# Expert products in groups of 512 tokens, with a transposed first product and rows turned by VectorE

## The chip, the cores and the metric

The kernel runs on one core of a Trainium2 chip. The metric is the device time of one execution in microseconds. Before the change it is 1199.97 us, the median of three runs (1203.39, 1199.97, 1197.99).

## What is computed

Two residual layers act on x, 8 batches of 512 tokens with 512 features, all in float32. The first (L0) makes a low-rank correction of a base matrix from a condition vector per batch and adds x times that matrix. The second (L1) is a mixture of experts: each token goes through a shared gated FFN (inner width 1024) and through two of eight experts (width 512), chosen by a router.

```
x  = x + L0(x)                                # 4096 tokens x 512
shared = silu(xf @ w1) * (xf @ w3) @ w2       # inner width 1024
s = sigmoid(concat(xf, tf) @ router_W)
topk_idx = top_k(s + router_bias, 2)          # gates: the two s, divided by their sum
h = gelu(xf @ W1e[e]);  y = h @ W2e[e]        # for each expert e, width 512
x = x + (shared + sum over 2 of gate * y) / 3
```

The router's bias is drawn with a spread of 1.126 and differs between experts by more than a sigmoid can; so two experts are chosen for all 4096 tokens. The kernel is written for any routing and reads the counts at run time.

## The kernel before, in words

All products run at float32 quality as three passes of TensorE: each operand is cut into a high part (a cast by ScalarE) and a low part (operand minus high part, by VectorE), and high x high, high x low and low x high are added in PSUM. That is `mm3`, L1375 to L1377; every product below has 3 matmuls for each 128 of its inner dimension, and two "cuts" for each operand.

Stages in order of time:
1. The L0 layer, batches 0 to 7, with the router beside it. Its result x1 is kept turned (features on partitions, `xp`) and is turned back by TensorE; `keep_tok` on ScalarE writes it as rows (`x1tok`). SP stores these rows in `x1_d`; GpSimd scatters each token's row twice into `xs_d`, one region per expert, in the order of the tokens (indirect DMAs, L701).
2. The shared FFN of the last batch (`ffn(S, ...)`), in 8 pieces h of 128 inner columns: 12 matmuls for U, 12 for V, and 12 for the sums of the piece before. Beside it VectorE makes the tables of tiles (`tables`, `rows_in_ys`, `gate_weights`), after its pieces 3 to 5. They go to a DRAM tensor and back into one partition, `tab_i`, from which the engines read registers (`value`).
3. The experts' tiles: 128 tokens of one expert each, as many as the counts need (a loop over pairs). SP fills up the rows of each expert's last tile with zeros (L577) ahead of it. Per tile: SP loads 128 rows of `xs_d` (L588, two buffers); TensorE turns them (`tx`, L1660, 4 transposes); ScalarE and VectorE cut them; TensorE multiplies them with the first weights, rows as the stationary operand (12 matmuls of 512 columns); ScalarE applies Gelu; TensorE turns the result (`th`, L1703, 4 transposes); both cut it; TensorE multiplies with the second weights (12 matmuls); VectorE copies the result out (L1297); SP stores it in `ys_d` (L604). GpSimd loads and cuts each active expert's weights once, ahead of its tiles, into one of two slots (`cut_expert`, L722 to L728).
4. The shared FFN of batches 0 to 6 in a loop (`ffn(F, ...)`). Beside it GpSimd gathers the two expert rows of each token (L752), and VectorE adds, in place in `xres`: x1 + shared/3 (`add_shared`) + gate x expert row twice (`add_expert`). SP stores the block. The last batch's sum, whose shared part is still in PSUM, is formed first.

Each engine executes its program in order and waits on semaphores at each instruction. PSUM banks `K[0]`, `K[1]`, `L`, `Rb` hold turned tiles and both products of stage 3; `M[0..3]` keep the last batch's shared sums meanwhile. Nothing plans the order at run time; it is as the code has it.

## Time and profile before

| | |
|---|---|
| median of 3 runs | 1199.97 us |
| profiled execution: time / span | 1202.75 us / 1200.9 us |
| TensorE busy | 1160.2 us (97%) |
| VectorE / ScalarE / GpSimd busy | 416.4 / 287.8 / 188.1 us |
| data moved | 151.82 MB, mean 126 GB/s |
| granted TensorE clock, mean | 0.985 of full speed |

The span is the time on the chip's engines, the time also holds what lies around it. A busy TensorE is not TensorE at its best: matmuls overlap, and the time from start to start tells what one costs. An engine's idle time counts only where something on the path waits for it.

### The profile page before, as it was taken

What the parts mean: (1) busy time and instruction counts of PE and PEld (TensorE: products, weight loads), DVE (VectorE), ACT (ScalarE), POOL (GpSimd) and SP (SyncE); (2) the same over time, 40 slices, a digit from 0 to 9 for tenths busy, and PEclk for the clock granted to TensorE, in tenths of its full rate; (3) what the DMA queues carried; (4) which work ended last, traced back from release to release, by engine and by line L of the source; (5) the groups of instructions that cost most, each with busy time, mean ns of one, the idle gap of its engine ahead of it and who ended that gap; (6) DMA issues with size and microseconds to landing.
All of it is one profiled execution on the core that took longest, in us unless ns stands there. A gap on an engine that the chain in (4) does not pass through costs nothing.

```text
span 1200.9 us, 18241 instructions
## 1 busy us (share of the span) xinstructions
PE 1160.2 (97%) x5762; PEld 935.4 (78%) x5763; DVE 416.4 (35%) x812; ACT 287.8 (24%) x498; POOL 188.1 (16%) x207
## 2 busy tenths in 40 slices
PE   6999898899999999999999998999999999999998
PEld 5666676778788888888888887888888888888887
DVE  4104653535233333333333334233333314233334
ACT  2212453521222222222222222121211112121211
POOL 2002165642510000000000003202020010202020
PEclk8999999899999999999999999999999999999999
DMA  8562589895332222222222224404031130404031
GB/s 309 227 239 95 207 299 347 289 306 162 129 118 83 79 87 79 79 87 79 82 84 83 83 79 123 175 1 175 1 100 74 39 136 0 175 0 175 0 125 49
DMA packets 70480, 151.82 MB, mean 126 GB/s; under 512 B 9753, under 2 KB 18457, under 8 KB 68658
## 3 DMA queue, kind: packets, MB, share of 16 engines
q1 hardware_dynamic: 57666, 111.55, 26.9%
q0 software_dynamic: 12784, 39.86, 9.4%
q8 instruction: 20, 0.33, 0.1%
q14 instruction: 10, 0.08, 0.0%
HBM read 88.73 MB, written 62.65 MB: 126 GB/s over the span
## 4 chain that ended last, share of the span: by engine, by line
PE 91%; DVE 4%; DMA 2%; POOL 1%; issue 1%; ACT 1%; SPq 0%; DVEq 0%; ACTq 0%
PE L L1375 7%; PE L L1377 7%; PE L L1376 7%; PE Rb L1377 7%; PE Rb L1375 7%; PE Rb L1376 7%; PE M L1375 5%; PE M L1376 5%; PE M L1377 5%; PE K L1376 5%; PE K L1375 5%; PE K L1377 5%; PE Rb L1465 3%; PE K L1703 2%; PE K L1660 2%; PE M L1403 2%
## 5 line engine op out<-in xcount | busy, mean ns | idle before, releaser
L752 POOL DMA_INDIRECT yb<-ys_d,pos_fix x64 | 61.2, 957 | 326.6 <-DVE xres L1324 308.6
L1375 PE MATMUL L<-weh,xgh 128*128 x260 | 107.6, 414 | 1.8 <-issue 1.8
L1276 DVE TENSOR_TENSOR xgl<-K,xgh 128x512 fp32r<-128x512 f32 x66 | 45.7, 692 | 173.4 <-ACT xgh L897 173.4
L1375 PE MATMUL Rb<-weh,hTh 128*128 x256 | 105.5, 412 | 0.0
L1375 PE MATMUL K<-x1h,w13h 128*128 128x512 f32 x256 | 101.6, 397 | 3.0 <-DVE x1l L1355 3.0
L1375 PE MATMUL M<-w2h,gTh 128*128 128x512 f32 x256 | 102.3, 399 | 2.3 <-DVE gTl L460 2.3
L1377 PE MATMUL L<-weh,xgl 128*128 x260 | 102.7, 395 | 0.0
L1376 PE MATMUL L<-wel,xgh 128*128 x260 | 102.5, 394 | 0.0
L1376 PE MATMUL K<-x1l,w13h 128*128 128x512 f32 x256 | 102.0, 398 | 0.0
L1376 PE MATMUL M<-w2l,gTh 128*128 128x512 f32 x256 | 101.9, 398 | 0.0
L1377 PE MATMUL M<-w2h,gTl 128*128 128x512 f32 x256 | 101.8, 398 | 0.0
L1377 PE MATMUL K<-x1h,w13l 128*128 128x512 f32 x256 | 101.7, 397 | 0.0
L1377 PE MATMUL Rb<-weh,hTl 128*128 x256 | 100.5, 393 | 0.0
L1376 PE MATMUL Rb<-wel,hTh 128*128 x256 | 100.2, 391 | 0.0
L445 ACT ACTIVATE slf<-K 128x512 f32<-128x512 f32 x64 | 38.3, 599 | 238.3 <-PE K L1377 234.2
L448 ACT CAST gTh<-slf 128x512 fp32r<-128x512 f32 x64 | 39.7, 621 | 191.7 <-DVE slf L458 191.7
L458 DVE TENSOR_TENSOR slf<-L,slf 128x512 f32<-128x512 f32 x32 | 22.1, 692 | 169.2 <-PE L L1377 162.5
L905 ACT CAST hTh<-K 128x512 fp32r<-128x512 f32 x65 | 38.2, 587 | 163.9 <-PE K L1703 163.9
L1297 DVE COPY yo<-Rb 128x512 f32<-128x512 f32 x64 | 44.3, 692 | 92.2 <-PE Rb L1377 92.2
L701 POOL DMA_INDIRECT xs_d<-x1tok,pos_int x64 | 68.2, 1065 | 38.0 <-issue 24.6
L901 ACT ACTIVATE hg<-L 128x512 f32<-128x512 f32 x65 | 38.9, 598 | 146.5 <-PE L L1377 146.5
L746 POOL COPY pos_fix<-ypos 128x8 int32 (+1 forms) x8 | 2.3, 283 | 442.6 <-DMA ys_d<-yo 390.0
(238 smaller groups left out, 2146.1 us busy)
## 6 DMA issues: line engine op xcount, KB each, us to landing
xr<-xs_d SPq DMA_DIRECT2D x68, 256.0 KB, 2.6
w2c<-in_L_cond_w_dram SPq DMA_DIRECT2D x8, 2048.0 KB, 8.5
ys_d<-yo SPq DMA_DIRECT2D x64, 256.0 KB, 2.1
xtok<-in_x_dram SPq DMA_DIRECT2D x32, 256.0 KB, 7.4
x_d<-x1tok SPq DMA_DIRECT2D x8, 1024.0 KB, 7.9
xres<-x_d SPq DMA_DIRECT2D x8, 1024.0 KB, 9.5
x1T_d<-xp SPq DMA_DIRECT2D x7, 1024.0 KB, 4.6
out_dram<-xres SPq DMA_DIRECT2D x7, 1024.0 KB, 4.8
```

The costliest lines, as they stand in the source:

```text
L445: nc.scalar.activation(slf[:, h % 2], U[h % 2][:], ACT.Silu).then_inc(ffn.silu, 1)
L448: nc.scalar.copy(gTh[:, h % 2], slf[:, h % 2]).then_inc(ffn.g_hi, 1)
L701: pool.indirect_dma_start(out=xs_d, out_offset=bass.IndirectOffsetOnAxis(ap=pos_int[:, c:c + 1].bitcast(U32), axis=0), in_=x1tok[i][:, t, ...
L752: pool.indirect_dma_start(out=yb[:, c, :], out_offset=None, in_=ys_d, in_offset=bass.IndirectOffsetOnAxis(ap=pos_fix[:, c:c + 1].bitcast(U ...
L901: nc.scalar.activation(hg[:], HP[:], ACT.Gelu).then_inc(h_g, 1)
L905: nc.scalar.copy(hTh[:].rearrange("p k n -> p (k n)"), TH[:]).then_inc(ht_hi, 1)
L1276: tt(xgl[:].rearrange("p k n -> p (k n)"), TX[:], xgh[:].rearrange("p k n -> p (k n)").bitcast(F32), ALU.subtract).then_inc(xg_lo, 1)
L1297: nc.vector.tensor_copy(yo[:, s], YP[:]).then_inc(y_sb, 1)
L1375: mm(o, ah, bh_, start=start, stop=False)
L1376: mm(o, ah, bl_, start=False, stop=False)
L1377: return mm(o, al, bh_, start=False, stop=stop)
L1465: last_mm = mm(Rb[32 * q:32 * q + 32, cc * P:(cc + 1) * P], hTz[:, k, 2 * j + part], w[:, k, 2 * q + j], start=(n == 0 and j == 0 and k == 0),
```

## The change

Stage 3 takes groups of 512 tokens (`GR`) instead of tiles of 128; regions, padding, tables and `ys_d` follow that size (`LAST` is the number of groups less one). For each group both weights of its expert are loaded whole by SP (1 MB each) and cut in four pieces by ScalarE and VectorE, also when the expert stays the same. The first product has the weights as stationary operand and all 512 tokens as moving one, so its result is already turned, four pieces of 128 hidden values in four banks; Gelu goes to `hg` in SBUF and is cut from there. The second product takes 128 tokens as stationary operand, in two halves of two banks. TensorE turns nothing in this stage. Instead `keep_tok` writes each row in the order (j, c, f) of its features (quarter j of every 128), SP loads quarter j of 512 rows onto partitions 32j to 32j+31 (four DMAs), and VectorE's 32x32 transposes of such a tile give features on partitions. ScalarE copies results out (`keep_y`). SP issues the padding of the regions after the tables; GpSimd zeroes the part of `ys_d` that groups may leave unwritten (7 groups) once the first weights are in. The final sums go to a tile of their own, `total`; the first add of each reads `xres` in the changed order, in four parts. In `tables` 17 operations stand where 35 did. ScalarE's and VectorE's cuts of the first group's first weights stand after piece 6 of stage 2.

```
+    GR = TT * P
+    REGION = N + GR
...
+        def groups(eng, body):
+            last = value(eng, LAST, 0, GROUPS_MAX - 1, 1)
+            with eng.Fori(0, last) as g:
+                body(g, g + 1)
+            body(last, None)
+            return last
...
+            pad_src = zeros[:].unsqueeze(1).broadcast_to([P, GR * D // (P * P), P])
+                row = value(sp, PAD, e, E * REGION - GR)
+                sp.dma_start(xs_d[ds(row, GR), :].rearrange("(p r) (k c) -> p (r k) c", p=P, c=P), pad_src).then_inc(pad_out, 16)
...
+            def load_e1(g):
+                row = value(sp, EROW, g, (E - 1) * KC)
+                sp.dma_start(e1raw[:], w1e_view[:, ds(row, KC), :]).then_inc(e1_in, 16)
...
+            def load_rows(g):
+                row = value(sp, ROW, g, E * REGION - GR)
+                rows = xs_d[ds(row, GR), :].rearrange("(n t) (j f) -> j t n f", t=32, j=4)
+                for j in range(4):
+                    sp.dma_start(xr[32 * j:32 * j + 32].rearrange("p t i f -> p (t i) f"), rows[j]).then_inc(xr_in, 16)
+            def store_y(g, s):
+                sp.wait_ge(y_sb, g * TT + (2 * s + 2 + Y_FREE))
+                alone(sp)
+                sp.dma_start(ys_d[ds(g * GR + s * (GR // 2), GR // 2), :].rearrange("(t p) d -> p t d", p=P),
+                             yo[:, 2 * s:2 * s + 2]).then_inc(y_out[s], 16)
...
+            load_e1(0)
+            sp.wait_ge(pad_out, 16 * E)
+            load_rows(0)
+            load_e2(0)
+            def load_group(g, n):
+                if n is not None:
+                    sp.wait_ge(e1_lo, n * KC)
+                    load_e1(n)
+                    sp.wait_ge(xt_f, n * TT)
+                    load_rows(n)
+                    sp.wait_ge(e2_lo, n * KC)
+                    load_e2(n)
+                else:
+                    sp.wait_ge(xt_f, g * TT + TT)
...
+                    sp.dma_start(xres[:], x1_view[:, (NB - 1) * TT:NB * TT, :]).then_inc(xres_in, 16)
+                    sp.wait_ge(h_ps, g * KC + KC)
+                    sp.wait_ge(xg_lo, g * TT + TT)
+                    alone(sp)
+                    sp.dma_start(x1raw[:], x1T_d[:, 0:1, :].rearrange("p b n -> p (b n)")).then_inc(x1raw_in, 16)
+                sp.wait_ge(ys_zero, 16 * (GROUPS_MAX - SURE))
+                store_y(g, 0)
+                store_y(g, 1)
...
+            pool.wait_ge(e1_in, 16)
+            zero_src = zeros[:].unsqueeze(1).broadcast_to([P, GR * D // (P * P), P])
+            for g in range(SURE, GROUPS_MAX):
+                pool.dma_start(ys_d[g * GR:(g + 1) * GR, :].rearrange("(p r) (k c) -> p (r k) c", p=P, c=P), zero_src
+                               ).then_inc(ys_zero, 16)
...
-                nc.scalar.copy(x1tok[TOK_BUFFER[b]][:, t], k_bank("t", b, t)[:]).then_inc(tok_sb, 1)
+                nc.scalar.copy(x1tok[TOK_BUFFER[b]][:, t].rearrange("p (j c f) -> p c j f", j=4, c=KC),
+                               k_bank("t", b, t)[:].rearrange("p (c j f) -> p c j f", j=4, c=KC)).then_inc(tok_sb, 1)
...
+            def cut_e1(g, m):
+                act.wait_ge(e1_in, g * 16 + 16)
+                if not first(g):
+                    act.wait_ge(h_ps, g * KC - KC + m + 1)
+                cols = slice(m * P, (m + 1) * P)
+                nc.scalar.copy(e1h[:, :, cols], e1raw[:, :, cols]).then_inc(e1_hi, 1)
+            def cut_e2(g, m):
+                act.wait_ge(e2_in, g * 16 + 16)
+                act.wait_ge(y_ps, g * TT + Y_FREE)
+                nc.scalar.copy(e2h[:, m], e2raw[:, m]).then_inc(e2_hi, 1)
+            def cut_x(g, t):
+                act.wait_ge(xt_f, g * TT + t + 1)
+                if first(g):
+                    act.wait_ge(S.v_ps, HC)
+                else:
+                    act.wait_ge(h_ps, g * KC)
+                nc.scalar.copy(x1h[:, :, t * P:(t + 1) * P], xt[:, t % 2]).then_inc(xg_hi, 1)
+            def gelu(g, m):
+                act.wait_ge(h_ps, g * KC + m + 1)
+                act.wait_ge(ht_lo, g * KC + (m - 1 + H_FREE))
+                nc.scalar.activation(hg[:, m % 2], G[m][:], ACT.Gelu).then_inc(h_g, 1)
+                act.wait_ge(h_g, g * KC + m + 1)
+                act.wait_ge(y_ps, g * TT + Y_FREE)
+                nc.scalar.copy(hTh[:, m], hg[:, m % 2]).then_inc(ht_hi, 1)
+            def keep_y(g, t):
+                act.wait_ge(y_ps, g * TT + (t + 1 + Y_FREE))
+                act.wait_ge(y_out[t // 2], g * 16 + YO_FREE)
+                nc.scalar.copy(yo[:, t], G[t][:]).then_inc(y_sb, 1)
...
+            after[HC - 2] = lambda: [cut_e1(0, m) for m in range(KC)]
+            ffn_act(act, S, 0, True, after)
+            act.sem_inc(y_sb, Y_FREE)
+            for t in range(TT):
+                cut_x(0, t)
...
+            def pass_group(g, n):
+                cut_e2(g, 0)
+                cut_e2(g, 1)
+                gelu(g, 0)
+                cut_e2(g, 2)
+                gelu(g, 1)
+                cut_e2(g, 3)
+                if n is not None:
+                    cut_e1(n, 0)
+                gelu(g, 2)
+                if n is not None:
+                    cut_e1(n, 1)
+                gelu(g, 3)
+                if n is not None:
+                    cut_x(n, 0)
+                    cut_e1(n, 2)
+                    cut_x(n, 1)
+                    cut_e1(n, 3)
+                    cut_x(n, 2)
+                    cut_x(n, 3)
+                keep_y(g, 0)
+                keep_y(g, 1)
+                if n is None:
+                    act.wait_ge(x1raw_in, 16)
+                    act.wait_ge(h_ps, g * KC + KC)
+                    cut_x1(0)
+                keep_y(g, 2)
+                keep_y(g, 3)
+            last = groups(act, pass_group)
...
+            def turn_rows(g, t):
+                dve.wait_ge(xr_in, g * 64 + 64)
+                if not (first(g) and t < 2):
+                    dve.wait_ge(xg_lo, g * TT + (t - 1))
+                nc.vector.transpose(xt[:, t % 2].rearrange("p c (i n) -> p i c n", i=4),
+                                    xr[:, t].rearrange("p i (c f) -> p i c f", c=KC)).then_inc(xt_f, 1)
+            def cut_x(g, t):
+                dve.wait_ge(xg_hi, g * TT + t + 1)
+                cols = slice(t * P, (t + 1) * P)
+                tt(x1l[:, :, cols], xt[:, t % 2], x1h[:, :, cols].bitcast(F32), ALU.subtract).then_inc(xg_lo, 1)
...
+            def pass_group(g, n):
+                cut_e2(g, 0)
+                cut_e2(g, 1)
+                cut_h(g, 0)
+                cut_e2(g, 2)
+                cut_h(g, 1)
+                cut_e2(g, 3)
+                if n is not None:
+                    turn_rows(n, 0)
+                    cut_e1(n, 0)
+                cut_h(g, 2)
+                if n is not None:
+                    turn_rows(n, 1)
+                    cut_e1(n, 1)
+                cut_h(g, 3)
+                if n is not None:
+                    cut_x(n, 0)
+                    cut_e1(n, 2)
+                    turn_rows(n, 2)
+                    cut_x(n, 1)
+                    cut_e1(n, 3)
+                    turn_rows(n, 3)
+                    cut_x(n, 2)
+                    cut_x(n, 3)
+            last = groups(dve, pass_group)
...
+            def fused(t, part, scale, n, done_):
+                if n is not None:
+                    dve.wait_ge(acc, n)
+                    ins = nc.vector.scalar_tensor_tensor(out=total[:, t], in0=part, scalar=scale, in1=total[:, t],
+                                                         op0=ALU.mult, op1=ALU.add)
+                else:
+                    for j in range(4):
+                        ins = nc.vector.scalar_tensor_tensor(
+                            out=total[:, t].rearrange("p (c j f) -> p j c f", j=4, c=KC)[:, j],
+                            in0=part.rearrange("p (c j f) -> p j c f", j=4, c=KC)[:, j], scalar=scale,
+                            in1=xres[:, t].rearrange("p (j c f) -> p j c f", j=4, c=KC)[:, j],
+                            op0=ALU.mult, op1=ALU.add)
+                ins.then_inc(done_, 1)
...
-            def tx(t, slot):
-                pe.wait_ge(xr_in[slot], ((t - slot) >> 1) * 16 + 16)
-                pe.wait_ge(xg_lo, t)
-                for k in range(KC):
-                    last_mm = nc.tensor.transpose(TX[:, k * P:(k + 1) * P], xr[:, slot, k * P:(k + 1) * P], ident[:])
-                last_mm.then_inc(xg_ps, 1)
...
-            def th(t):
-                pe.wait_ge(h_g, t + 1)
-                pe.wait_ge(ht_lo, t)
-                for k in range(KC):
-                    last_mm = nc.tensor.transpose(TH[:, k * P:(k + 1) * P], hg[:, k * P:(k + 1) * P], ident[:])
-                last_mm.then_inc(ht_ps, 1)
...
+            def mm1(g):
+                pe.wait_ge(xg_lo, g * TT + TT)
+                for m in range(KC):
+                    pe.wait_ge(e1_lo, g * KC + m + 1)
+                    pe.wait_ge(y_sb, g * TT + (m - TT + 1 + Y_FREE))
+                    cols = slice(m * P, (m + 1) * P)
+                    for k in range(KC):
+                        last_mm = mm3(G[m][:], e1h[:, k, cols], e1l[:, k, cols], x1h[:, k], x1l[:, k], k == 0, k == KC - 1)
+                    last_mm.then_inc(h_ps, 1)
+            def mm2(g):
                 for s in range(2):
+                    for m in range(KC):
+                        if s == 0:
+                            pe.wait_ge(ht_lo, g * KC + (m + 1 + H_FREE))
+                            pe.wait_ge(e2_lo, g * KC + m + 1)
+                        for t in (2 * s, 2 * s + 1):
+                            if m == 0:
+                                pe.wait_ge(h_g, g * KC + t + 1)
+                            rows = slice(t * P, (t + 1) * P)
+                            last_mm = mm3(G[t][:], hTh[:, m, rows], hTl[:, m, rows], e2h[:, m], e2l[:, m], m == 0, m == KC - 1)
+                            if m == KC - 1:
+                                last_mm.then_inc(y_ps, 1)
...
```

`load_e2`, `cut_e1`, `cut_e2` and `cut_h` on VectorE follow the same pattern (high part awaited, then one subtraction). SP's `load_group` for the last group loads `xres` and the first block's input instead of a next group.

## Rows read from the trace of the kernel before

**Rows 1.** Page, part 4: chain that ended last, share of the span by engine.
```profile
PE 91%; DVE 4%; DMA 2%; POOL 1%; issue 1%; ACT 1%; SPq 0%; DVEq 0%; ACTq 0%
```

**Rows 2.** Windows: length, busy of PE, PEld, DVE, ACT, POOL; PEclk, DMA share, GB/s.
```profile
0.00:244.30 244.30, 214.18 (x1432) 166.04 (x1434) 95.17 (x294) 80.96 (x141) 82.78 (x110) 0.95 0.70 253
244.30:305.70 61.40, 59.10 (x248) 46.99 (x247) 29.16 (x80) 14.57 (x21) 25.19 (x18) 0.97 0.66 213
305.70:725.50 419.80, 414.72 (x2069) 343.14 (x2068) 135.00 (x196) 109.47 (x198) 16.65 (x8) 1.00 0.27 88
725.50:1200.90 475.40, 472.19 (x2016) 379.24 (x2016) 157.07 (x243) 82.83 (x139) 63.48 (x72) 1.00 0.24 84
```

**Rows 3.** Timeline of PE in the tiles: start us, us, engine line op.
```profile
600.56 0.60 PE L1703 MATMUL K<-ident,hg 128*128 128x128 f32 x4
603.76 0.60 PE L1660 MATMUL K<-ident,xr 128*128 128x128 f32 x4
604.11 0.48 PE L1375 MATMUL Rb<-weh,hTh 128*128 x1
606.95 0.60 PE L1703 MATMUL K<-ident,hg 128*128 128x128 f32 x4
```

**Rows 4.** Groups by line, PE: count | busy, mean ns | idle before.
```profile
L1660 PE MATMUL K<-ident,xr 128*128 128x128 f32 x264 | 39.4, 271 | 0.0
```

**Rows 5.** Timeline of PE in the first FFN block.
```profile
732.75 0.40 PE L1375 MATMUL K<-x1h,w13h 128*128 128x512 f32 x1
735.55 0.40 PE L1375 MATMUL Rb<-x1h,w13h 128*128 128x512 f32 x1
```

**Rows 6.** Timeline of PE: idle before in brackets, and the matmuls behind it.
```profile
311.80 0.49 PE L1375 MATMUL L<-weh,xgh 128*128 x1 [1.83 <-issue]
313.32 0.63 PE L1377 MATMUL L<-weh,xgl 128*128 x1
313.75 0.63 PE L1375 MATMUL L<-weh,xgh 128*128 x1
725.53 0.58 PE L1375 MATMUL K<-x1h,w13h 128*128 128x512 f32 x1 [3.02 <-DVE x1l L1355]
```

**Rows 7.** Timeline of ACT and PE at the end of the shared FFN.
```profile
291.76 0.62 ACT L448 CAST gTh<-slf 128x512 fp32r<-128x512 f32 x1 [3.02 <-DVE slf L458]
302.83 0.50 PE L1375 MATMUL M<-w2h,gTh 128*128 128x512 f32 x1 [0.28 <-DVE gTl L460]
```

**Rows 8.** Timeline of DVE: first and last of 35 operations of the tables.
```profile
267.80 0.16 DVE L956 SCALAR_TENSOR_TENSOR tw<-iota,taken 128x8 f32<-128x8 f32 x1
274.67 0.17 DVE L996 CAST tabi<-tab 128x8 int32<-128x8 f32 x1
```

**Rows 9.** SP timeline; windows: zeros alone, long rows; DMA issues with landing.
```profile
278.78 14.04 SPq L577 DMA_DIRECT2D xs_d<-zeros  x8
...
270.00:271.00 1.00, 1.00 (x6) 0.82 (x5) 0.83 (x6) 0.00 (x0) 0.00 (x0) 1.00 0.97 288
298.00:299.00 1.00, 1.00 (x6) 0.82 (x5) 0.00 (x0) 0.00 (x0) 0.00 (x0) 1.00 1.01 406
...
xs_d<-zeros SPq DMA_DIRECT2D x9, 256.0 KB, 3.4
```

**Rows 10.** DMA issues: count, KB each, us from issue to landing.
```profile
weraw<-in_L_cond_W1e_dram POOLq DMA_DIRECT2D x2, 1024.0 KB, 6.0
```

**Rows 11.** Groups by line: ACT Gelu, DVE subtraction, DVE 32x32 transposes.
```profile
L901 ACT ACTIVATE hg<-L 128x512 f32<-128x512 f32 x65 | 38.9, 598 | 146.5 <-PE L L1377 146.5
...
L1276 DVE TENSOR_TENSOR xgl<-K,xgh 128x512 fp32r<-128x512 f32 x66 | 45.7, 692 | 173.4 <-ACT xgh L897 173.4
L1165 DVE STREAM_TRANSPOSE zz<-L 32x128 f32<-32x128 f32 x32 | 10.0, 313 | 0.6
```

**Rows 12.** Timeline of DVE at the last block's seventh piece.
```profile
1186.08 5.39 DVE L1324 SCALAR_TENSOR_TENSOR xres<-yb,gate_fix,xres 128x512 f32<-128x512 f32 x8
1192.22 0.69 DVE L458 TENSOR_TENSOR slf<-Rb,slf 128x512 f32<-128x512 f32 x1 [0.75 <-PE Rb L1377]
```

More of the change, by code:

```diff
@@ L950, in tables @@
             tt, ts, red = nc.vector.tensor_tensor, nc.vector.tensor_scalar, nc.vector.tensor_reduce
-            cnt, nt, active, ends, ranks, past, rows, t7, t8, t9 = (tw[:, i] for i in range(10))
-            col = [tab[:, i:i + 1] for i in range(8)]
-            tmp = [tw[:, 10, i:i + 1] for i in range(4)]
-            ti = [twi[:, 1, i:i + 1] for i in range(4)]
+            cnt, nt, ends, past, rows, t9 = (tw[:, i] for i in (0, 1, 2, 3, 4, 9))
+            col = [tab[:, i:i + 1] for i in range(COLS)]
@@ L960, in tables @@
             link(nc.vector.tensor_copy(nt, twi[:, 0]))
[L961 removed]
             link(nc.vector.tensor_tensor_scan(ends, ones[:, 0:E], nt, 0.0, ALU.mult, ALU.add))
[L963 removed]
             link(ts(past, ends, iotap[:, 0:1], None, ALU.is_le))
[L966 removed]
+            link(red(tmp[1], past, AX, ALU.add))
```

353 lines of the change are left out of this document (113 added, 240 removed).

## The prediction, made before the changed kernel ran

> **What bounds the kernel now.** I read the chain of waits first: 91% of the path to the end is TensorE [rows 1]. The windows then cut the span by stage: everything ahead of the shared FFN takes 244.3 us, the shared FFN 61.4, the expert tiles 419.8 and the seven FFN blocks behind them 475.4 [rows 2]. TensorE is busy in 414.7 of the 419.8 us of the expert stage, VectorE in 135, ScalarE in 109, and the DMA engines are a quarter used. So in this stage only what TensorE itself executes, or a wait put in front of it, moves the end.
>
> The timeline of TensorE in that stage shows the tile: from one group of turned hidden values (L1703) to the next are 6.39 us [rows 3], and the stage issues 64 of these tiles (the 64 stores of one tile each, and 264 input transposes with the two tiles read ahead [rows 4], say the same). Inside a tile are 24 matmuls of 512 columns and 8 transposes of 128 columns; four transposes hold the engine 0.35 us (603.76 to 604.11, [rows 3]). In the FFN blocks the same form of matmul, weights at a fixed address, comes every 0.2333 us (12 from 732.75 to 735.55, [rows 5]). GpSimd loaded and cut weights for two experts only (two loads of each kind, [rows 10]). Two experts with 64 full tiles are 4096 tokens each, thus 8 groups of 512 each, 16 groups with no padding; other routing would cost a part group per expert.
>
> **The change, part by part.** The sum is made against the profiled execution: 1200.9 us span, 1202.75 us time, so 1.85 us lie outside the span. That run is 2.8 us over the median of the runs shown, 1199.97.
>
> *Removed from TensorE: the transposes.* The input rows are turned by VectorE, and a first product with the weights stationary gives hidden values already turned. The number of 512-column matmuls stays: per group 48 and 48, in all 16 x 96 = 1536. At 0.2333 us that is 22.4 us a group and 358.4 us in all. The tiles' matmuls run a little closer inside a tile, 24 in 6.39 - 2 x 0.35 = 5.69 us with the joints, 0.237 each, so no loss is taken; if the new ones came every 0.2275 us, the sum would be 9 less. Stage before 419.8, now 358.4: 61.4 saved at most. Of that 50 are the transposes' 64 x 0.79, 2.8 the 65th first product that ran ahead for nothing, 3.0 the wait at the stage's end, 1.8 one near its start, and two stretches of about 8 matmuls after these at a spacing of 0.43 us (granted clock at the lower level, [rows 6]), 1.6 each.
>
> *Added ahead of the stage: 8 MB of zero rows.* Each expert's end is padded with 512 rows instead of 128, for all eight experts, and the first group's rows wait for it; before, 2 MB. The tables are ready at 274.8 [rows 8]; they lose some 18 of their 35 links of 0.2 us, so 271.2 now. From there to the first pad were 3.9 us [rows 8, 9]: first pad at 275.1. Zero rows move in 512-byte pieces, and where they have the engines for themselves these carry 288 GB/s at a full share [rows 9]. 8 x 1,048,576 bytes take 29.1 us. A 256 KB zero store lands 3.4 us after its issue, of which 0.9 is data, so 2.5 on top: 306.7. SP issues the load of the first weights only behind this, on the same queue: 2.6 us more at the 406 GB/s of a load with long rows [rows 9], so 309.3.
>
> Now the queues behind that wait. ScalarE is told to cut these weights between the shared FFN's seventh and eighth piece, that is after 292.4 [rows 7]; it waits 17 us, and its Silu of the eighth piece stands behind. Four casts of 0.6, then Silu, product, cast, subtraction: 309.3 + 2.4 + 0.6 + 0.7 + 0.6 + 0.7, with the gaps 315.1. TensorE, which went on at 302.8 before (waiting 0.28 only [rows 7]), has its last 12 matmuls of this stage at 315.1, at the lower clock until 320.2. Meanwhile SP waits for the pads, loads the rows (1 MB; they share the engines with 7 MB of zeros that GpSimd now starts), landing about 316.5; four turns, casts and subtractions in sequence at 0.69 with hand-overs take 5.9: the first expert matmul at 322.4, against 305.7. That is 16.7 us lost, and 1.6 for the clock. Bounds: nothing, if the pads are quicker than I think or the wait lies elsewhere; 25 us, if GpSimd's zeros take half of the engines from the rows all the time.
>
> *The loop.* ScalarE has 24 instructions of 0.6 us a group and VectorE 20 of 0.7: 14.4 and 14 us of 22.4 [rows 11], covered if the order fits. I follow one group, its first product at 0: pieces of hidden values come at 2.8, 5.6, 8.4 and 11.2; the second product starts at 11.2 and wants the third and fourth piece at 14.0 and 15.4. On VectorE "turn rows of the next group, cut a weight piece" stands twice ahead of these (turn, cut, cut_h, turn, cut, cut_h): from the landing of the rows the two cut_h end after 2.1 and 4.1 us. So rows have to be there by 11.3, or TensorE waits for the difference. SP reaches the loads only after the store of the previous group's last half, about 1.4, reads a register, and issues the weights at about 2.7. A 1 MB weight load landed 6.0 us after issue [rows 10]: 8.7; the rows stream behind it, 3.6 us at 288 GB/s: 12.3. With less neighbouring traffic than that load had, 10.8. I take 12.0, a wait of 0.7 us, in 15 groups 10.5 us. Ends: zero; and if each of the four quarter loads needs the 1.75 us at which 256 KB zero stores followed each other (14.04 us for eight [rows 9]), 7.0 in place of 3.6, a wait of 4.4.
> The turn is priced from the VectorE transpose that the trace has, 0.313 us for 128 columns on 32 partitions [rows 11]: 0.69 if it streams like a subtraction of 512 columns, 1.25 if four times the small one. The nearer row is the subtraction of the same size; at 1.25 the second cut_h is 1.1 later, which belongs into the same range.
> The row view shows full-partition zeros at 288 GB/s; no row shows a large transfer on 32 partitions, which is what each quarter load is. The Trainium skill, "SBUF — State Buffer", section "Door 1: The DMA port swizzle", says that a transfer over 32 partitions reaches 8 of 16 ports, and gives 189 GB/s for 1 MiB against 328 over all. By the page's figure the rows would stream in 5.5 us instead of 3.6 (an estimate), a wait of 2.6 a group and 39 us in place of 10.5.
>
> *Zeros of GpSimd.* 7 MB of zeros and 4 MB of loads share the engines from 309 on; at 288 GB/s that ends near 348, and the first result store (about 342), with the loads of group 2 behind it on SP, waits for that: 1 us. The two weight loads per group in place of two in all raise the traffic from 88 to about 190 GB/s, well under the 406 seen; TensorE does not see it but for the above.
>
> *The end of the stage and the blocks.* Input for the first FFN block is loaded and cut during the last second product, so the 3.0 us wait goes, and the clock does not fall: the blocks take 475.4 - 1.6. The first add of each sum goes in four parts (16 instructions of 0.28 for 4 of 0.69): 2 us more on VectorE, hidden under 5.6 us of products, but in the last block VectorE's sums of 5.39 become about 7.2 where only 0.75 us were free [rows 12]; 1.1 late, of which TensorE has 0.4 of slack: 0.7. The reordered write of the turned tokens, and 2 MB of zeros that SP no longer issues earlier, I cost at nothing: GpSimd's scatter sets that stretch.
>
> *Sum:* 1200.9 - 61.4 + 16.7 + 1.6 + 10.5 + 1.0 - 1.6 + 0.7 = 1168.4; plus 1.85 is 1170.3, against 1202.75; from the median of 1199.97 the same step gives **1167**.
>
> **The rivals.**
> A. *The pads do not hold the start.* 18.3 us come back, 1149, and with no wait in the loop 1138. For it: the eight pads of before landed within 3.4 us each. Against it: 29 us of bytes in a stretch of 27 us.
> B. *The rows come late in every group.* Each us of landing past 11.3 is one of TensorE, 15 times. If the row load takes 5.5 us, between the 3.6 and the 7.0 above, it lands at 13.9, the wait is 2.6 and the 15 cost 28.5 us more than my 10.5: 1196. With half of that excess, 1181. For it: single buffers for rows and weights, loaded only after the previous store. Against: the DMA engines have a quarter of their time in use now [rows 2] and half then. The page of the Trainium skill named above would make this the case.
> C. *The same, and the clock falls each time*: the slower side. After a wait of 1.8 us TensorE ran 8 matmuls at 0.43 instead of 0.23 [rows 6], 1.6 us. From the point where one wait in a group is 1.8 us, a group loses 3.4 and 15 lose 51: without my 10.5 the sum is 1156.6, so 1208, and more beyond; the four loads at 1.75 us would give 4.4 + 1.6 = 6.0 a group and 1247. For it: nothing shows a quarter load's price. Against: the lateness splits over two pieces of hidden values, and each wait must be long by itself; waits of 0.25 to 0.28 us left the clock at the higher level.
> D. *The change does not take the work off TensorE*, if the first product with stationary weights needed more matmuls: excluded by the code, 48 for 48.
>
> **How the numbers follow.** Forecast 0.45 (1155 to 1178), A 0.15, B 0.27, C 0.13. A difference under 0.5%, 6 us, can't be told from none here. C is slower in most of its part (0.09), within 0.5% in the rest (0.02), to which B's far end adds 0.04: same 0.06, slower 0.09, faster 0.85. The range from 1143 to 1200 leaves out a part of A and C.
>
> **What would show it.** Right: no 128-column transposes of TensorE in the stage; first expert matmul near 322 with ScalarE waiting for the weights' DMA from 292 to 309; groups every 23.1 us with VectorE's turn waiting for the row DMA; no wait of 3 us before the first block. Wrong: a first expert matmul before 310, a turn far from 0.69 us, groups over 24 us, a fallen clock inside the loop.

## The result, and the profile after

The changed kernel took 1213.41 us (median of 4, 1211.64 to 1215.86) beside 1200.96 for the kernel before on the same chip (4 runs, 1197.99 to 1203.39). The ratio is 1.0106, with a 95% interval from 1.0075 to 1.0137: a little slower. Forecast were 1167 us, in a range that ended at 1200; rival C, the slower side, had 1208. The profiled execution spans 1212.4 us.

Part 4 of the page after, the chain that ended last, and three groups of part 5 (count | busy, mean ns | idle before and who ended it):
```profile
PE 67%; DMA 14%; SPq 7%; DVE 7%; issue 4%; ACT 2%; DVEq 0%; ACTq 0%
...
L1445 PE MATMUL M<-w2h,gTh 128*128 128x512 f32 x256 | 102.2, 399 | 16.0 <-DVE gTl L475 16.0
L1445 PE MATMUL K<-e2h,hTh 128*128 128x512 f32 x128 | 58.8, 460 | 55.0 <-DVE hTl L1318 54.3
L1298 DVE STREAM_TRANSPOSE xt<-xr 128x512 f32<-128x512 f32 x64 | 45.1, 705 | 109.3 <-DMA xr<-xs_d 109.1
```
TensorE had 91% of the path before [rows 1] and has 67% now; DMA has 14%. The transposes of TensorE are gone, and VectorE's turn of a tile costs 0.705 us, as taken. But TensorE idles 54.3 us in the groups of the experts in front of the second product, in 15 stretches, and 16 us ahead of the first group; VectorE idles 109 us for the row load.

The stages after, to be held against [rows 2] (length, busy of PE, PEld, DVE, ACT, POOL; PEclk, DMA share, GB/s):
```profile
0.00:244.00 244.00, 217.58 (x1456) 168.61 (x1457) 99.46 (x299) 84.23 (x146) 84.66 (x115) 0.97 0.72 260
244.00:303.00 59.00, 48.16 (x208) 38.71 (x206) 17.43 (x54) 8.35 (x13) 5.97 (x8) 0.94 0.80 237
303.00:741.00 438.00, 376.98 (x1549) 302.03 (x1550) 205.35 (x336) 221.36 (x391) 7.98 (x7) 0.93 0.62 170
741.00:1212.40 471.40, 467.88 (x2016) 378.64 (x2015) 160.35 (x328) 82.69 (x138) 62.84 (x72) 1.00 0.24 84
```
The third window, the expert stage with the last matmuls of the shared FFN, holds 520 fewer matmuls than before and TensorE is busy 37.7 us less in it, yet it is 18 us longer. Its granted clock is 0.93 instead of 1.00.

**The start.** Timeline of SyncE (SP), ScalarE and TensorE around the pads (start us, us, engine, line; in brackets the idle time before and who ended it):
```profile
266.31 24.87 SPq L586 DMA_DIRECT2D xs_d<-zeros  x8
293.58 1.29 SPq L597 DMA_DIRECT2D e1raw<-in_L_cond_W1e_dram  x1
298.99 1.94 SPq L608 DMA_DIRECT2D xr<-xs_d  x4
...
302.63 2.18 ACT L904 CAST e1h<-e1raw 128x512 fp32r<-128x512 f32 x4 [20.11 <-DMA e1raw<-in_L_cond_W1e_dram]
...
307.81 0.80 PE L1445 MATMUL M<-w2h,gTh 128*128 128x512 f32 x1 [15.66 <-DVE gTl L475]
314.47 0.47 PE L1445 MATMUL K<-x1h,e1h 128*128 128x512 f32 x1 [1.17 <-DVE x1l L1304]
```
The first expert matmul comes 53.0 us after the tables (261.48); I had 322.4 - 271.2 = 51.2. The 24.9 us are SyncE's issuing; the zero rows themselves move at 284 GB/s from 268 to 292, so 8 MB take 29.5 us.

**Group 0.** GpSimd's zeros, the row load of group 1 (SyncE) and the turn that waits for it:
```profile
302.90 8.08 POOL L736 DMA_DIRECT2D ys_d<-zeros  x7 [51.20 <-DMA e1raw<-in_L_cond_W1e_dram]
...
313.86 8.95 SPq L608 DMA_DIRECT2D xr<-xs_d  x4
...
341.04 0.71 DVE L1298 STREAM_TRANSPOSE xt<-xr 128x512 f32<-128x512 f32 x1 [18.26 <-DMA xr<-xs_d]
```
The rows of group 1 need 27 us from the first issue to the turn, and TensorE waits 14.7.

**A later group**, g = 5; SyncE, VectorE and TensorE (first the matmul that opens the group), then windows between the landings:
```profile
455.83 4.38 SPq L613 DMA_DIRECT2D ys_d<-yo  x2
462.07 0.40 SPq L597 DMA_DIRECT2D e1raw<-in_L_cond_W1e_dram  x1
463.39 2.16 SPq L608 DMA_DIRECT2D xr<-xs_d  x4
...
473.64 0.71 DVE L1298 STREAM_TRANSPOSE xt<-xr 128x512 f32<-128x512 f32 x1 [6.64 <-DMA xr<-xs_d]
474.27 0.65 DVE L1309 TENSOR_TENSOR e1l<-e1raw,e1h 128x512 fp32r<-128x512 f32 x1
474.84 0.68 DVE L1318 TENSOR_TENSOR hTl<-hg,hTh 128x512 fp32r<-128x512 f32 x1
...
458.78 0.39 PE L1445 MATMUL K<-x1h,e1h 128*128 128x512 f32 x1
...
475.58 0.50 PE L1445 MATMUL K<-e2h,hTh 128*128 128x512 f32 x1 [3.04 <-DVE hTl L1318]
...
465.00:467.00 2.00, 2.00 (x11) 1.65 (x10) 1.29 (x2) 1.16 (x3) 0.00 (x0) 1.00 1.02 357
467.00:469.00 2.00, 2.00 (x11) 1.65 (x10) 0.00 (x0) 0.81 (x2) 0.00 (x0) 1.00 1.19 199
469.00:471.00 2.00, 2.00 (x10) 1.67 (x9) 0.00 (x0) 1.94 (x4) 0.00 (x0) 1.00 1.24 196
```
This is the order that the prediction followed: store, weights, rows, turn, cut of a weight piece, cut of hidden values. The turn of the rows starts 14.9 us after the group does (14.65 on average over the groups behind group 0); 11.3 were needed, and TensorE waits 3.04. While the weights load the engines move 357 GB/s; while only rows load, 196 to 199 with the engines shown just as full.

Behind such a wait the clock falls in nine of the groups 1 to 14 and stays in five (2, 5, 8, 10 and 13). Group 4 is one of the nine; the rows are TensorE's timeline (spacing 0.23 us before, 0.43 after), a window of two of these microseconds, and the windows of groups 4 and 5 as a whole:
```profile
448.60 0.50 PE L1445 MATMUL K<-e2h,hTh 128*128 128x512 f32 x1 [2.66 <-DVE hTl L1318]
...
451.84 0.63 PE L1445 MATMUL K<-e2h,hTh 128*128 128x512 f32 x1
452.27 0.63 PE L1446 MATMUL K<-e2l,hTh 128*128 128x512 f32 x1
...
451.00:453.00 2.00, 2.00 (x6) 1.61 (x5) 2.00 (x4) 0.62 (x1) 0.00 (x0) 0.50 0.00 0
432.18:458.78 26.60, 23.85 (x98) 18.91 (x96) 12.45 (x20) 13.68 (x25) 0.00 (x0) 0.94 0.56 158
458.78:484.33 25.55, 22.36 (x97) 17.86 (x96) 12.45 (x20) 13.56 (x25) 0.00 (x0) 1.00 0.59 152
```
The granted clock is 0.50 from 451 to 453, the lower of the two levels. The nine groups with such a stretch take 26.5 us on average and the five without it 25.3, so the fall costs 1.2 us each time, 11 us in all.

### The profile page after: what moved, and what is told of

It is laid out like the page before. It is cut to its first block, busy times and chain, and to the rows that moved or that the text cites. A ratio compares the mean times of both kernels' runs of the same rounds, so it can differ in the third digit from the quotient of the medians.

```text
span 1212.4 us, 15385 instructions
## 1 busy us (share of the span) xinstructions
PE 1110.6 (92%) x5226; PEld 888.0 (73%) x5226; DVE 482.6 (40%) x1015; ACT 396.6 (33%) x687; POOL 161.4 (13%) x200
## 4 chain that ended last, share of the span: by engine, by line
PE 67%; DMA 14%; SPq 7%; DVE 7%; issue 4%; ACT 2%; DVEq 0%; ACTq 0%
DMA xr<-xs_d 12%; PE K L1445 7%; PE K L1446 6%; PE K L1447 6%; PE M L1445 4%; PE M L1446 4%; PE M L1447 4%; PE L L1445 4%; PE L L1446 4%; PE L L1447 4%; PE Rb L1446 3%; PE Rb L1445 3%; PE Rb L1447 3%; SPq L419 3%; PE Rb L1535 3%
## 5 line engine op out<-in xcount | busy, mean ns | idle before, releaser
L1445 PE MATMUL K<-e2h,hTh 128*128 128x512 f32 x128 | 58.8, 460 | 55.0 <-DVE hTl L1318 54.3
L1298 DVE STREAM_TRANSPOSE xt<-xr 128x512 f32<-128x512 f32 x64 | 45.1, 705 | 109.3 <-DMA xr<-xs_d 109.1
L1445 PEld LDWEIGHTS K<-e2h,hTh 128*128 128x128 f32 x128 | 27.4, 214 | 70.7 <-DVE hTl L1318 65.3
L917 ACT CAST x1h<-xt 128x512 fp32r<-128x512 f32 x64 | 39.7, 620 | 115.1 <-DVE xt L1298 115.1
L1445 PEld LDWEIGHTS M<-w2h,gTh 128*128 128x128 f32 x256 | 48.6, 190 | 28.6 <-DVE gTl L475 16.8
L1314 DVE TENSOR_TENSOR e2l<-e2raw,e2h 128x512 fp32r<-128x512 f32 x64 | 42.6, 687 | 64.0 <-ACT e2h L909 64.0
L473 DVE TENSOR_TENSOR slf<-Rb,slf 128x512 f32<-128x512 f32 x32 | 22.1, 691 | 114.0 <-PE Rb L1447 114.0
L1318 DVE TENSOR_TENSOR hTl<-hg,hTh 128x512 fp32r<-128x512 f32 x64 | 43.9, 687 | 51.8 <-ACT hTh L925 51.8
L475 DVE TENSOR_TENSOR gTl<-slf,gTh 128x512 fp32r<-128x512 f32 x64 | 44.3, 692 | 47.5 <-ACT gTh L463 47.5
L1473 PE MATMUL M<-xTh,bh 128*128 128x512 f32 x128 | 56.4, 441 | 6.0 <-DVE bl L1129 3.2
```

The source lines that it names most:

```text
L473: nc.vector.tensor_tensor(slf[:, h % 2], V[h % 2][:], slf[:, h % 2], ALU.mult).then_inc(ffn.g_f, 1)
L475: nc.vector.tensor_tensor(gTl[:, h % 2], slf[:, h % 2], gTh[:, h % 2].bitcast(F32), ALU.subtract).then_inc(ffn.g_lo, 1)
L1298: nc.vector.transpose(xt[:, t % 2].rearrange("p c (i n) -> p i c n", i=4), xr[:, t].rearrange("p i (c f) -> p i c f", c=KC)).then_inc(xt_f, 1)
L1314: tt(e2l[:, m], e2raw[:, m], e2h[:, m].bitcast(F32), ALU.subtract).then_inc(e2_lo, 1)
L1318: tt(hTl[:, m], hg[:, m % 2], hTh[:, m].bitcast(F32), ALU.subtract).then_inc(ht_lo, 1)
L1445: mm(o, ah, bh_, start=start, stop=False)
```

## The experiments

"Rest" below is the span from the store of the tables (`tab_d<-tabi`) to the end: it leaves out the part ahead, which differs by chip and execution (runs 7 to 9). It is 926.0 us for the kernel before and 950.9 for the changed one. "Period" is the mean time from one row load to the next over 13 groups behind group 1: 26.09 us in the changed kernel. The kernel before took 1201.94 us in the set of runs 1 to 4, 1215.11 in that of runs 5 to 8, 1217.22 in that of runs 9 to 11 and 1196.08 in that of run 12, so each time is held against the kernel before of its own set. Most edits are in SyncE's program.

**1. Rows over 128 partitions in pieces of 2 KB.** The features then reach the products in another order, so the result is another one; the work is the same.
```
-  rows = xs_d[ds(row, GR), :].rearrange("(n t) (j f) -> j t n f", t=32, j=4)
+  rows = xs_d[ds(row, GR), :].rearrange("(t p) d -> t p d", p=P)
-  sp.dma_start(xr[32 * j:32 * j + 32]..., rows[j])
+  sp.dma_start(xr[:, j].rearrange("p i f -> p (i f)"), rows[j])
```


> The row load is four transfers of 128 rows over all 128 partitions in pieces of 2 KB, instead of four over 32 partitions in pieces of 512 bytes; all else stays, the same bytes move and the same turns run, but the features reach the products in another order (this part of the computation is changed). Theory T1, the quarter loads' low rate holds the loop: the rows stream at the 365 to 400 GB/s of a weight load, 2.7 us instead of 5.5 for 1 MB, so they land some 2.8 us sooner after the group's start (about 11.8 instead of 14.6), TensorE's wait before the second product's third piece falls from 2.7-3.0 us to about 0.5, the clock does not fall inside the loop, groups take about 22.3 us instead of 26.1 and the time is 1213 - 14 x 3.8 = 1160. Rival R1, SyncE's order (the loads queued behind the result store) alone: landing moves by less than 1 us and the time stays above 1195. Rival R2, the order on VectorE or ScalarE: landing moves by 2.8 us but the wait stays above 2 us, time above 1200.

Measured: 1150.46 us (2 runs; ratio to before 0.9588, 0.9516 to 0.9659), rest 887.1, period 22.40. SyncE's row load, VectorE's turn and TensorE's waits:
```profile
459.45 1.97 SPq L608 DMA_DIRECT2D xr<-xs_d  x4
...
466.52 0.71 DVE L1298 STREAM_TRANSPOSE xt<-xr 128x512 f32<-128x512 f32 x1 [3.46 <-DMA xr<-xs_d]
...
PE K L1445 <- DVE hTl L1318: 6.2, 2, 6.0
```
From issue to turn the rows take 7.07 us instead of 10.25 (463.39 to 473.64). The wait is gone but for 6.0 us in group 0 and 0.2 in one other, and the clock stays at the higher level in groups 1 to 15. With the same bytes, order and turns, 64 us of the rest come back, 52 of them in groups 1 to 14: T1.

**2. The same with pieces of 512 bytes.**
```
+  rows = xs_d[ds(row, GR), :].rearrange("(t p) (j f) -> j p t f", p=P, j=4)
+  sp.dma_start(xr[:, :, j], rows[j])
```


> The row load is four transfers over all 128 partitions, each in pieces of 512 bytes as in the changed kernel (the features reach the products in another order; this part of the computation is changed). It tells the number of partitions apart from the size of the pieces. If the 32 partitions are what is slow (T1): streaming at about the 288 GB/s that zero stores of 512-byte pieces have, 3.6 us for 1 MB instead of 5.5, landing 1.9 us sooner, groups about 23.3 to 24 us, time 1170 to 1185. If the 512-byte pieces are what is slow (R3): rows land at about 14.6 us after the group's start as now, groups 26 us, time 1205 to 1215.

Measured: 1170.06 us (0.9751, 0.9679 to 0.9823), rest 907.5, period 23.35.
```profile
470.87 2.22 SPq L608 DMA_DIRECT2D xr<-xs_d  x4
...
479.38 0.71 DVE L1298 STREAM_TRANSPOSE xt<-xr 128x512 f32<-128x512 f32 x1 [4.91 <-DMA xr<-xs_d]
...
PE K L1445 <- DVE hTl L1318: 24.9, 15, 13.3
```
8.51 us from issue to turn here, more than in most groups of this run. On average over groups 2 to 15 it is 10.03 us in the changed kernel, 8.03 here and 7.10 in run 1. So of the 2.9 us between the changed kernel and run 1, the 32 partitions make 2.0 and the short pieces 0.9. The size of the pieces (R3) is not the main cause, and not nothing. Waits of 0.5 to 1.5 us are left in groups 1 to 14, and behind none of them does the clock fall.

**3. No pads.** The eight stores and the wait for them are deleted.

> The eight pad stores (8 MB of zero rows) and the wait for them are left out; this input has full groups only, so nothing else changes. If the pads hold the start (the prediction's step, 16.7 + 1.6 us): ScalarE's cut of the first expert's weights waits no more, the first expert matmul comes at 296 to 300 instead of 314.5 and the time falls by 14 to 18 us, to 1195-1199. If the zeros of GpSimd (7 MB), which then start sooner, take over: less than 8 us gained.

Measured: 1186.75 us (0.989, 0.9818 to 0.9962), rest 924.4: 26.5 us less, more than either case said. The first expert matmul comes 35.7 us after the tables (296.48) instead of 53.0, and in group 0 the row loads are 30.8 us apart (44.3 before), since the zeros of GpSimd start at 272, 30 us sooner. In the loop the waits stay (TensorE's waits; groups 1 to 14 together take 369 us, 366 in the changed kernel):
```profile
PE K L1441 <- DVE hTl L1314: 44.2, 15, 3.4
```
15 waits of 2.9 on average, none of 14.7.

**4. Weights loaded once.** `load_e1(n)` and `load_e2(n)` and their waits are deleted from the pass.

> The weight loads of all groups but the first are left out (the cuts stay, the second expert's tokens are multiplied by the first's weights; this part of the computation is changed): 15 x 2 MB less traffic, and SyncE reaches the row load right after the result store without a 1 MB weight transfer ahead of it. T1 (with the rows behind the weights on the same engines): rows land 2.5 to 3.5 us sooner, the wait before the second product goes below 0.5 us, groups about 22.2 us, time 1155 to 1165. If the quarter loads alone are slow for another reason than what stands ahead of them: landing at about +12, as well, but group 0's loss of 17 us stays in any case, since it comes from the 7 MB of zeros. If ScalarE or VectorE hold the loop: groups stay near 26 us.

Measured: 1151.03 us (0.9592, 0.9511 to 0.9674), rest 887.0, period 21.77. Row load and turn:
```profile
460.88 1.95 SPq L608 DMA_DIRECT2D xr<-xs_d  x4
...
468.34 0.71 DVE L1294 STREAM_TRANSPOSE xt<-xr 128x512 f32<-128x512 f32 x1 [2.55 <-DMA xr<-xs_d]
```
With no weights ahead the quarter loads take 7.46 us (7.51 on average), longer than the 7.10 of run 1 behind 1 MB of weights. It is the sum of the two, weights ahead and a low rate, that is late; taking either away is enough. The groups behind group 0 take 21.8 us; TensorE keeps one wait, 11.7 us in group 0.

**5. Zeros for the results ahead of the shared FFN.** The loop of seven stores moves from GpSimd to SyncE, before `sp.wait_ge(weff_ps, 1)`.

> The 7 MB of zeros for the result rows are issued by SyncE before the shared FFN, where the DMA engines are little used, instead of by GpSimd when the first expert's weights have landed; otherwise the changed kernel. If these zeros, sharing the engines with the loads of group 1 and with the first result store, cause group 0's loss of 17 us (38.9 us instead of 21.8; theory T2): group 0 takes 26 us like the others, TensorE's longest wait inside the loop falls from 14.7 to about 3, time 1213 - 13 to 15 = 1198 to 1200. Rival: the single buffers alone hold group 0 (the same wait as in each later group, plus the first-time order of the queues): less than 3 us gained. If the zeros disturb the conditioning loads where they are now put, up to 5 us are given back.

Measured: 1237.5 us beside 1215.11 for the kernel before on that chip; rest 940.6, 10.3 less than the changed kernel's. TensorE's waits:
```profile
PE K L1445 <- DVE hTl L1318: 44.6, 14, 3.9
...
PE M L1485 <- DMA SB<-xwh_d: 7.6, 1, 7.6
```
The row loads of groups 1 and 2 are 27.8 us apart instead of 44.3, and group 0 takes 21.8 us instead of 39.0, so T2 is right for group 0. The groups behind it ran at a period of 26.7 and gave 7 us of that back. Ahead of the tables TensorE waits 7.6 us for a conditioning load, a wait that the changed kernel does not have and more than I allowed. The time came out 38 us above the forecast, mainly because the tables come at 293.3 instead of 261.5; on this chip they come late in every kernel profiled (283.8 to 293.5).

**6. Loads one pass ahead.**
```
+ sp.wait_ge(e1_lo, KC);  load_e1(1);  sp.wait_ge(xt_f, TT);  load_rows(1)
  def load_group(g, n):
-   sp.wait_ge(e1_lo, n * KC);       load_e1(n)
-   sp.wait_ge(xt_f, n * TT);        load_rows(n)
    sp.wait_ge(e2_lo, n * KC);       load_e2(n)
+   sp.wait_ge(e1_lo, n * KC + KC);  load_e1(n + 1)
+   sp.wait_ge(xt_f, n * TT + TT);   load_rows(n + 1)
    store_y(g, 0);  store_y(g, 1)
```
The loads of the pass before the last reach past the last group and are not used; the last pass waits for them.

> SyncE issues the weight and row loads of group n+1 as soon as their buffers are free in group n, ahead of the stores of group n's results, instead of one pass later behind them; no buffer is added, the same bytes move, the quarter loads stay as they are. If lateness is what counts (T1: rows land 3.3 us too late, whether by their rate or by their start): they now land before the previous group's last third, the wait of 2.7 to 3 us goes in all groups, the clock stays, groups take 21.8 us: 14 x 4.2 = 59 us less, and group 0's loss stays (it comes from the zeros): about 1155. Rival R1a: the loads now meet the result stores and the second expert's weights and are as late as before: time above 1195. Rival R2: the order of VectorE or ScalarE makes the wait: groups stay above 24 us, time above 1185.

Measured: 1178.05 us beside 1215.11 for the kernel before on that chip, ratio 0.9692 (0.9628 to 0.9756); rest 889.1, 61.8 less. SyncE's pass, the window of one group, and TensorE's wait:
```profile
441.19 0.39 SPq L597 DMA_DIRECT2D e1raw<-in_L_cond_W1e_dram  x1
442.51 2.08 SPq L608 DMA_DIRECT2D xr<-xs_d  x4
444.94 2.45 SPq L613 DMA_DIRECT2D ys_d<-yo  x2
455.10 0.40 SPq L601 DMA_DIRECT2D e2raw<-in_L_cond_W2e_dram  x1
...
397.00:419.00 22.00, 22.00 (x99) 18.22 (x98) 12.78 (x21) 13.47 (x24) 0.00 (x0) 1.00 0.67 191
...
PE K L1451 <- DVE hTl L1324: 13.1, 1, 13.1
```
The loads stand ahead of the store, TensorE is busy throughout at full clock, and every group behind group 0 takes 21.76 us. The quarter loads are about as slow as they were (median 7.0 us to land, 7.3 in the changed kernel): what cost was that they came late.

**7 and 8. The kernel before with the other spacing of the experts' regions** (`REGION = N + 4 * P`), **and unchanged.**

> The kernel before with one number changed: the rows set aside for each expert in the scattered tokens are 4608 instead of 4224, as in the changed kernel (9.44 MB instead of 8.65 MB from expert to expert). It asks where the 10 us come from that the changed kernel gains ahead of the expert stage, in code that is nearly the same. If the spacing of the experts' regions makes the scattered writes of GpSimd and the weight loads beside them slower: the wait of TensorE at 213 us falls from 7.1 to about 3.7 and the time falls by 5 to 10 us. If it is the order of the copied tokens (4 parts of rows), the queue of zeros that SyncE no longer has at 256 us, or chance: within 2 us of before in that wait.

> The kernel before, unchanged, profiled once more: how much the part ahead of the expert stage differs from one execution to another. If the 10 us by which the changed kernel's shared FFN ends sooner are chance: the wait at 213 us (7.1 us) and the end of that stage (about 302) move by several us here. If they belong to the change: the wait is 7 us and the end 302 within 1 us.

The ratio of run 7 is 0.9992 (0.9956 to 1.0027). The tables are stored at:
```profile
283.82 0.35 SPq L571 DMA_DIRECT2D tab_d<-tabi  x1
```
in run 7, and in run 8, which is the kernel before word for word:
```profile
293.49 0.35 SPq L571 DMA_DIRECT2D tab_d<-tabi  x1
```
In the trace of before it was 274.87. The rest is 925.5 and 927.2 (926.0 before). So the part ahead of the tables differs by 10 us between two executions on one chip, of kernels whose median times agree, and the rest does not. The spacing does not matter.

**9. The changed kernel again.**

> The changed kernel itself, once more, to be held against the others of this set on the same chip. In the set before, on another chip, the part ahead of the tables (261.5 us in the trace of the changed kernel) took 284 to 294 us in the kernel before and 290 to 293 in versions of the changed one, while all that follows the tables agreed within 2 us with the first chip (926.0, 925.5 and 927.2 us for the kernel before). So: from the tables to the end 951 us within 3, wherever the tables come; before 926. If the changed kernel really gains ahead of the tables, they come about 10 us sooner than in the kernel before here too; if that gain was chance, the ratio is above 1.015.

Measured: 1240.85 us beside 1217.22, ratio 1.0195 (1.0124 to 1.0267); tables at 284.74, rest 952.4, as expected. From the medians, with the rest and the 1.85 us outside the span taken off, the tables stand at 289.4 before and 286.6 after here, and at 273.1 and 260.7 on the first chip. The gain ahead of the tables is thus 12 us there, 3 here, and none between run 6 and its neighbour before. What sets it stays open.

**10. The first weights ahead of the pads** (with the loads of run 6).
```
  load_e1(0)
+ load_e2(0)
+ (the eight pad stores)
  sp.wait_ge(pad_out, 16 * E)
  load_rows(0)
```


> The loads one pass ahead (as in the prefetch version), and the first group's weights are issued ahead of the eight pad stores instead of behind them; correct for any routing. ScalarE's cut of the first weights then waits no more and TensorE's wait of 15.7 us before the end of the shared FFN goes; the first rows still wait for the pads. But GpSimd's zeros start with the weights' landing, 30 us sooner, and share the engines with the pads. T1/T2: 15 MB in a row at 337 GB/s end some 45 us after the tables as pads alone would after 25; first expert matmul 5 to 15 us later than the 53 us after the tables that the changed kernel shows at worst, or 10 us sooner at best; group 0's loss of 13 to 17 us mostly gone. From the tables to the end 889 (prefetch) - 5 to - 20: 870 to 885. Rival: the pads and zeros together hold the start longer than before: above 889.

Measured: 1193.09 us (0.9791, 0.9736 to 0.9846), rest 904.9: the rival. The start of the weights releases GpSimd's zeros into the pads:
```profile
293.59 55.29 SPq L617 DMA_DIRECT2D xs_d<-zeros  x8
...
PE K L1451 <- DVE x1l L1310: 50.1, 1, 50.1
```
55.3 us for the eight issues instead of 24.9, and one wait of 50.1. The 337 GB/s of the expectation is 8 MB over SyncE's 24.9 us of issuing, which end before the data; pads and zeros together moved 283 GB/s from 300 to 350, at which 15 MB take 56 us and not 45. The groups behind take 21.76 us as in run 6.

**11. The same, zeros by SyncE**: four before the shared FFN, three behind the last token store.

> As the version with the first weights ahead of the pads, and the 7 MB of zeros issued by SyncE: four before the shared FFN (the engines idle from 88 to 104 us), three behind the last token store ahead of the tables. Correct for any routing. T2: no wait before the last piece of the shared FFN, first expert matmul about 10 us sooner than with the changed kernel, group 0's loss gone, groups 21.8 us: from the tables to the end 951 - 60 - 14 - 10 = 867 to 872, of which up to 5 us may be given back ahead of the tables by the zeros there. Time 25 to 35 us below the prefetch version. Rival: the zeros delay the conditioning loads or the tables by more than 8 us, so nothing is won over the prefetch version.

Measured: 1168.24 us beside 1217.22, ratio 0.9603 (0.9551 to 0.9656); rest 881.1, where I expected 867 to 872. TensorE's one wait inside this part:
```profile
339.66 0.77 PE L1454 MATMUL K<-x1h,e1h 128*128 128x512 f32 x1 [26.26 <-DVE x1l L1313]
```
59.7 us after the tables: the pads start 11 us after them, not 5, since the tables' own two transfers stand behind zeros and two weight loads stand ahead. This version is faster than both kernels and keeps the pads, which inputs with part groups need.

**12. The same without the eight pads.**

> The version before (loads one pass ahead, first weights first, zeros by SyncE) without the eight pad stores; one 1 MB store of zeros at the end of the last region stays for the row load that runs past the last group. Its output is right for inputs with full groups only, as this one; it shows what the pads cost once all else is mended. If the pads alone hold the first expert matmul at 60 us after the tables: it comes at about 36 us after them, the end of the shared FFN, as in the version without pads, and from the tables to the end 881 - 24 = 857 us. If the three stores of zeros ahead of the tables and the two weight loads now hold the first rows: 865 or more.

Measured: 1119.55 us beside 1196.08 in this set (1217.22 in the set of runs 9 to 11, on a chip of the same number), ratio 0.9357 (0.9334 to 0.938); rest 852.9. The tables are ready on VectorE before SyncE, still issuing zeros, stores them:
```profile
260.64 0.17 DVE L1028 CAST tabi<-tab 128x4 int32<-128x4 f32 x1
...
263.73 4.26 SPq L586 DMA_DIRECT2D tab_d<-tabi  x1
...
296.73 0.47 PE L1451 MATMUL K<-x1h,e1h 128*128 128x512 f32 x1 [2.42 <-DVE x1l L1310]
```
The first expert matmul comes 33.0 us after this store and 35.9 after the tables are ready, so counted from there the rest is 855.8: the pads cost 25 us once all else is mended (28 by the store). Against the kernel before the gain is 76 us; 70 of them lie behind the ready tables, the others in the part ahead, which is not to be counted on.

## Why the prediction was wrong

By its own steps, the profiled execution against the 1168.4 of the sum:

| stretch | predicted | measured | difference |
|---|---|---|---|
| start to the tables | 271.2 | 261.5 | -9.7 |
| tables to the first expert matmul | 51.2 | 53.0 | +1.8 |
| group 0, with the zeros and the clock | 25.7 | 39.0 | +13.3 |
| groups 1 to 14 | 14 x 23.1 = 323.4 | 14 x 26.11 = 365.6 | +42.2 |
| last group and seven blocks | 496.9 | 493.3 | -3.6 |
| sum | 1168.4 | 1212.4 | +44.0 |

- **The step that failed: "the rows stream behind it, 3.6 us at 288 GB/s: 12.3 ... I take 12.0, a wait of 0.7 us".** The mechanism was right, the size was not. The weights landed near the 8.7 us that I had (their cut starts 9.0 us after the group's start on average, 9.4 in group 5); the rows then took 5.6 us (5.45 in group 5, 468.19 to 473.64), so 14.65, and the wait was 2.83 on average (54.3 - 14.7 over 14). My rule, every us past 11.3 is one of TensorE, gives 3.35 for 14.65; the five groups whose clock stayed lost 3.6 against 21.76 (25.34 on average). I used the rate of a transfer over all partitions for one over 32, with no row for the latter, and took the nearest row by size of piece. For a load over all partitions that row was near: in run 2 the same 512-byte pieces take 3.9 us behind the weights, in run 1 the long ones 3.0. Runs 1, 2, 4 and 6 confirm it from four sides.
 What I set beside the sum, the Trainium skill, "SBUF — State Buffer", section "Door 1: The DMA port swizzle" (32 partitions reach half of the ports, 189 GB/s for 1 MiB), is borne out: 196 to 199 GB/s here, 5.45 us where 5.5 followed from it. Its figure is for one transfer of 1 MiB, and the rate here is that of four of 256 KB in a row.
- **The clock.** The 42.2 us of groups 1 to 14 are 14 x (2.83 - 0.7) = 29.8 of wait, 14 x (26.11 - 21.76 - 2.83) = 21.3 beside it, less 14 x 0.64 = 8.9 for closer matmuls. Of the 21.3 some 11 are the lower clock, 1.2 us in each of nine groups. The others are 0.74 us in every group: a second wait of about 0.3 us, for the fourth piece of hidden values, and a slower first matmul behind each wait. This is rival C, which I gave 0.13, holding that each wait had to be long by itself. They were: 2.66 and 3.04 in the rows above. B's own wait of 2.6 was already past the 1.8 us from which C lets the clock fall, so the split between the two was unsound. C was not wholly right either: it had the clock fall in every group at 1.6 us. That its 1208 lies near the 1213 measured is partly luck, since group 0 took 11 us more than C allows and the part ahead of the tables 10 less.
- **"Zeros of GpSimd ... 1 us" was the second step that failed: group 0 took 13 us more than the sum had.** I asked when the last zero lands and which store waits for it. What counted was the load of group 1 that queues among them: 27 us from issue to turn. Run 5 (17 us of group 0 gone) and run 3 (13) show it. My own bound for the start, "if GpSimd's zeros take half of the engines from the rows", named the effect for group 0's rows, a place too early.
- **Pads: right**, 53.0 us from the tables where I had 51.2, with ScalarE's wait of 20.1 (17), TensorE's of 15.7, and zeros at 284 GB/s (288). Run 3 gave 17.3 us back at the start, where the prediction had 18.3 with the clock. Rival A was wrong.
- **Right too:** the turn at 0.69 (0.705); no wait and no lower clock ahead of the blocks; the last block, where the two sums take 7.0 us (7.2) and TensorE waits 0.3 (0.7). The last group and the blocks together came 3.6 less, nearly all by closer matmuls: a block takes 66.8 us instead of 67.2.
- **Closer matmuls.** In run 6, where nothing waits, 96 matmuls take 21.76 us, 0.2267 each instead of 0.2333; the 9 us that I named for this case and left out of the sum came.
- **The part ahead of the tables** ended 9.7 us sooner than the sum had it, for no reason that I can show; by runs 6 and 9 it isn't to be counted on, and on the chip of run 9 the change reads 2% slower.

So the 61.4 us were saved where I said, by the balance of the span (1212.4 - 1200.9 = 11.5). The start (53.0 us from the tables instead of 30.9), group 0 (39.0 instead of 21.8) and the loop (14 x 4.35) took 100 back; the closer matmuls (10), the blocks (471.6 for 475.4) and the part ahead of the tables (13) returned 27. In run 12 none of the three losses is left, for inputs that need no pads.

## What to carry to other kernels

A transfer's price depends on how many partitions it touches: where the trace has no transfer of that shape, price it by its own worst row and say what the loop would then do, above all if a wait of 2 to 3 us would also lower the clock. With single buffers, ask for each load when its buffer is free, and issue it there, ahead of the stores: that was worth 62 us with the slow loads left as they were. Bulk stores of zeros that nobody reads soon still cost: here they stood in front of the next loads, and group 0 took 39.0 us with them and 21.8 without.

## What the runs showed of the hardware that I had not expected

- A load of 1 MB in four parts over 32 partitions each took 7.5 us on average from issue to use with no weights ahead of it, 10.0 behind 1 MB of weights; over 128 partitions, behind the same weights, 8.0 in pieces of 512 bytes and 7.1 in pieces of 2 KB. The DMA share reads 1.19 to 1.24 while only the quarter loads move: the engines look full at 196 to 199 GB/s, where 357 went while the weights were still loading.
- A wait of 2.66 us was followed by matmuls at 0.43 us, one of 3.04 us was not: the group at 475.58 went on at 0.23. Of the 14 waits of 2.66 to 3.28 us in groups 1 to 14 nine were followed by the lower clock, and their lengths overlap with those of the other five. So the length of the wait alone does not decide, and what does no run here shows.
- Matmuls of 512 columns came every 0.2267 us in the groups of run 6, every 0.2333 in the FFN blocks of the kernel before and every 0.2320 in those of the changed kernel, all at the higher clock. The cause was not tested.
- SyncE's issuing itself takes longer when the engines have much to do: four quarter loads were issued in 1.94 us ahead of group 0 and in 8.95 behind GpSimd's zeros.
